# A decoder layer on one core: separate instruction orders for ramp, loop and drain, earlier loads of x, and the split of the norms moved to GpSimd

## The reference

```python
# 1. linear attention, 16 heads of 16, 64 random features
q, k, v = split(x @ Wq.T + bq), split(x @ Wk.T + bk), split(x @ Wv.T + bv)
def phi(u):                       # norm: the squared norm of each head's q or k
    norm = sum(u * u) / (2 * sqrt(16))
    return (exp(u @ orf.T / 16 ** 0.25 - norm) + 1e-6) / 8
kv, ksum = phi(k).T @ v, phi(k).sum(rows)
attn = (phi(q) @ kv) / (phi(q) @ ksum) @ Wo.T + bo
x = layernorm(x + attn)
# 2. softmax attention: queries from ctx_1024, keys x, values ctx_1024
x = layernorm(x + softmax_attention(k=ctx_1024, q=x, v=ctx_1024))
# 3. gated FFN with ternary weights and 8-bit activations
x = layernorm(x + bitlinear(silu(bitlinear(x, w_gate)) * bitlinear(x, w_up), w_down))
```

## Time and profile before

| | |
|---|---|
| median of three runs | 504.94 us |
| the profiled execution | 507.6 us |
| its span, first to last instruction | 505.9 us |
| mean granted TensorE clock | 0.972 |
| busy: TensorE / VectorE / ScalarE / GpSimd | 86% / 89% / 85% / 72% |
| tiles | 32 |

### The profile page before, as it was taken

One profiled execution on the slowest core, in us unless ns is written; L12 is line 12 of the kernel. 1 busy time (PEld: TensorE's weight loads), 2 busy tenths in 40 slices (PEclk: granted clock), 3 DMA queues, 4 the chain that ended last, 5 costly groups with the idle time before them and its releaser, 6 DMA issues.

```text
span 505.9 us, 18665 instructions
## 1 busy us (share of the span) xinstructions
PE 437.2 (86%) x6566; PEld 304.7 (60%) x6566; DVE 450.7 (89%) x1355; ACT 429.1 (85%) x908; POOL 365.0 (72%) x789
## 2 busy tenths in 40 slices
PE   4568888889899999999999999999999988866541
PEld 2235666666677667677767776777777766543220
DVE  4667786889999999999999999999999998999771
ACT  2247788979999999999999999999999998866632
POOL 1447766768888888888888888888888876754332
PEclk9979899999999999999999999999999999999975
DMA  7666556776666666666666666666666777532212
GB/s 180 235 127 110 121 125 116 110 136 94 137 136 140 137 142 138 139 140 145 145 145 145 145 135 141 136 138 143 137 140 130 136 137 138 76 74 53 54 42 62
DMA packets 192644, 64.07 MB, mean 127 GB/s; under 512 B 172384, under 2 KB 192352, under 8 KB 192608
## 3 DMA queue, kind: packets, MB, share of 16 engines
q1 hardware_dynamic: 190080, 60.46, 58.2%
q10 hardware_dynamic: 2528, 3.15, 1.7%
HBM read 17.31 MB, written 4.19 MB: 43 GB/s over the span
## 4 chain that ended last, share of the span: by engine, by line
PE 56%; ACT 15%; DMA 11%; DVE 7%; issue 5%; POOL 3%; SPq 1%; ACTq 0%; POOLq 0%; DVEq 0%
PE bank L1129 11%; PE bank L1333 8%; PE bank L1360 4%; PE bank L1304 3%; PE bank L1181 3%; PE bank L1223 3%; DMA tT<-pkT 3%; DMA ffn_ld<-in_L_ffn_w_down_dram 3%; ACT pT L629 3%; PE bank L1143 3%; ACT pT L628 2%; DMA tT<-nmT 2%; PE bank L1238 2%; PE bank L1320 2%; ACT x L556 2%
## 5 line engine op out<-in xcount | busy, mean ns | idle before, releaser
L1129 PE MATMUL bank<-wq_hi,xT 128*128 128x512 f16 (+1 forms) x256 | 72.1, 337 | 4.0 <-DVE vv L814 2.6
L432 POOL TENSOR_TENSOR ve<-mv,lneps 128x1 f32<-128x1 f32 x96 | 19.2, 200 | 67.8 <-DVE mv L864 52.7
L436 POOL TENSOR_TENSOR rs<-ve,mhalf 128x1 f32<-128x1 f32 x96 | 54.7, 569 | 0.0
L628 ACT ACTIVATE pT<-bank 128x512 f32<-128x512 f32 x64 | 37.9, 592 | 12.6 <-PE bank L1294 10.6
L944 DVE SCALAR_TENSOR_TENSOR g<-th,bank 128x512 f32<-128x512 f32 x64 | 42.9, 671 | 3.9 <-ACT th L651 3.7
L556 ACT ACTIVATE x<-y,nmr,rs 128x256 f32<-128x256 f32 x64 | 39.8, 621 | 7.4 <-DVE y L1005 3.8
L895 DVE TENSOR_REDUCE negm<-bank 128x4 f16<-128x512 f32 x64 | 43.5, 679 | 2.8 <-PE bank L1258 2.7
L896 DVE TENSOR_REDUCE negm<-bank 128x4 f16<-128x512 f32 x64 | 43.6, 681 | 0.0
L1360 PE MATMUL bank<-downT,hqT 128*128 128x256 bf16 x256 | 34.3, 279 | 10.3 <-DMA hqT<-hq 10.3
L575 ACT ACTIVATE phk<-bank 128x512 f32<-128x512 f32 x64 | 39.3, 616 | 4.6 <-PE bank L1148 4.6
L1129 PE MATMUL bank<-wq_lo,xT 128*128 128x256 f16 (+1 forms) x128 | 43.0, 336 | 0.0
(11 more groups left out here) (184 smaller groups left out, 1574.7 us busy)
## 6 DMA issues: line engine op xcount, KB each, us to landing
xs<-in_x_dram SPq DMA_DIRECT2D x32, 128.0 KB, 2.2
cs<-in_ctx_dram SPq DMA_DIRECT2D x32, 128.0 KB, 2.2
xr<-in_x_dram SPq DMA_DIRECT2D x32, 128.0 KB, 2.2
out_dram<-ot SPq DMA_DIRECT2D x32, 128.0 KB, 1.8
ffn_ld<-in_L_ffn_w_gate_dram ACTq DMA_DIRECT2D x1, 1024.0 KB, 8.7
ffn_ld<-in_L_ffn_w_up_dram ACTq DMA_DIRECT2D x1, 1024.0 KB, 11.5
ffn_ld<-in_L_ffn_w_down_dram ACTq DMA_DIRECT2D x1, 1024.0 KB, 13.7
pkAT<-pkA SPq DMA_TRANSPOSE x64, 3.2
```

The source lines that it names most:

```text
L436: g.tensor_tensor(rs[n - 1][:, :], ve[n - 1][:, :], mhalf[:, :], ALU.pow).then_inc(done[f"pw{n}"], 1)
L628: sc.activation(pT[:, grp, 0, :, :], even.rearrange("p (c t) -> p c t", c=4), ACT.Exp, scale=0.25)
L1129: last = T.matmul(o, xT[:, 2 * part + c, :], w[:, c, cols], start=(n == 0), stop=(n == 5))
```

## The change

Seven things change together.

1. `run` takes three functions per engine. `ramp(i)` and `drain(i)` call the steps through `lead(step, i, lag, until)` and `trail(step, i, lag, since)`, each in an order of its own; `iteration` keeps a third order for the loop and two iterations ahead of it. The ramp goes up to tile 13 or so, the loop to tile 29 or so.
2. The loop's order changes on every engine, and the lags of some steps become one smaller (for example `phk0` on TensorE from 3 to 2, `x1_` on ScalarE from 5 to 4).
3. `nhi` and `nlo` go from VectorE to GpSimd.
4. SyncE issues x of tile 0 first, then the projection weights, then x of tile 1, the biases, the output weight and its bias, and the gate matrix. `w_down` and `w_up` follow on SyncE too, after the load of x of tile 3, which waits for `xlo` of tile 1. ScalarE issues none of them any more.
5. VectorE clears all its buffers at the start, ahead of `wq_lo`; the first `wq_lo` comes before the wait for the small weights.
6. The PSUM banks are assigned anew, and the waits that guard them are written for the new orders: by tile number in ramp and drain (`only_at`), in the loop by `wait_looped`. In TensorE's loop the waits of `qkm`, `vm`, `xTp`, `st0`, `kvs`, `s0`, `tm` and others name other steps than before.
7. Steps that lacked a semaphore get one (`s1`, `hq0`), and waits on them are added.

```diff
-            def iteration(i, par): ... run(eng, iteration, lags, first)
+        def run(eng, ramp, iteration, drain, ramps, first, last, drains):
+            for i in range(*ramps):
+                ramp(i)
+            iteration(first - 2, 0)
+            iteration(first - 1, 1)
+            with eng.Fori(first, last - 1, 2) as i:
+                iteration(i, 0)
+                iteration(i + 1, 1)
+            for i in range(*drains):
+                drain(i)
...
+            def load_first(t):
+                sp.dma_start(xs[:, t, :], x[t]).then_inc(moved["x"][t], 16)
+
+            load_first(0)
             for n, w in enumerate((Wq, Wk, Wv)):
                 sp.dma_start(wld[:, n, :, :], w.rearrange("(o p) i -> p o i", p=P)).then_inc(w_in[n], 16)
+            load_first(1)
...
+            def ramp(i):                                # SyncE
+                once(load_gate, i, -78)
...
+                once(load_output, i, -94)
...
+                lead(load_x, i, -68, 16)
...
+                once(load_down, i, -65)
+                lead(load_c, i, -64, 13)
+                once(load_up, i, -65)
...
+                lead(kT, i, -65, 14)
...
+            def nhi(t, par):                            # GpSimd
+                wait_ahead(pool, t, par, ("nr", 0), landings=(("kT", -1), ("qT", -1),))
+                g.tensor_scalar(norm_hi, nrm[:, :, :], 1.0, 0.0, ALU.mult, ALU.add).then_inc(done["nhi"], 1)
+
+            def nlo(t, par):
+                wait(pool, "nhi", t)
+                g.tensor_tensor(norm_lo, nrm[:, :, :], norm_hi, ALU.subtract).then_inc(done["nlo"], 1)
...
             def iteration(i, par):                      # GpSimd
...
+                go(rs3, i, par, 11)
+                go(phe, i, par, 3)
+                go(nf, i, par, 1)
+                go(rs2, i, par, 7)
+                go(chi, i, par, 4)
+                go(clo, i, par, 4)
+                go(nhi, i, par, 1)
+                go(xb_, i, par, 3)
+                go(rs1, i, par, 4)
+                go(lo, i, par, 1)
+                go(nlo, i, par, 1)
...
             def iteration(i, par):                      # VectorE
+                go(bs1, i, par, 4)
+                go(rd, i, par, 3)
+                go(y1, i, par, 4)
+                go(at, i, par, 3)
+                go(am, i, par, 7)
+                go(y3, i, par, 10)
+                go(ac, i, par, 7)
+                go(hc, i, par, 8)
+                go(ar, i, par, 7)
+                go(hr, i, par, 8)
+                go(qnt, i, par, 7)
+                go(hs, i, par, 8)
...
+            def ramp(i):                                # VectorE
...
+                once(magnitudes[2], i, -9)
...
+                lead(qk_, i, -10, 12)
...
+                once(magnitudes[0], i, -11)
...
+                once(magnitudes[1], i, -9)
...
+                lead(nr, i, -10, 12)
...
             def iteration(i, par):                      # ScalarE
...
+                go(ot_, i, par, 11)
+                go(p1, i, par, 6)
+                go(nT_, i, par, 3)
+                go(p0, i, par, 6)
+                go(x2_, i, par, 7)
```

More of the change, by code:

```diff
@@ L263, in wait_ahead, with looping, wait_looped, only_at @@
                     eng.wait_ge(semaphore, v)
+        def looping(t):
+            return not isinstance(t, int)
+        def wait_looped(eng, name, t, off=0):
+            if looping(t):
+                eng.wait_ge(done[name], t + off + 1)
+        def only_at(eng, t, tile, name, producer_tile):
+            if isinstance(t, int) and t == tile:
+                eng.wait_ge(done[name], producer_tile + 1)
+        def lead(step, i, lag, until):
+            t = i - lag
+            if 0 <= t < until:
+                step(t, t % 2)
+        def trail(step, i, lag, since):
+            t = i - lag
+            if since <= t < TILES:
+                step(t, t % 2)
         def go(step, i, par, lag):
             t = i - lag
-            if not isinstance(t, int) or 0 <= t < TILES:
-                step(t, (par + lag) % 2)
+            step(t, (par + lag) % 2)
         def once(step, i, at):
@@ L490, in iteration @@
+            def iteration(i, par):
                 go(xhi, i, par, 0)
+                go(xlo, i, par, 0)
                 go(rs3, i, par, 11)
-                go(rs1, i, par, 5)
-                go(xqf, i, par, 8)
-                go(lo, i, par, 2)
-                go(hq0, i, par, 9)
-            run(pool, iteration, 11, 12)
+                go(phe, i, par, 3)
[8 more added lines that the diff above has]
+                go(nlo, i, par, 1)
+                go(xqf, i, par, 7)
+                go(hq1, i, par, 8)
+                go(hq0, i, par, 8)
+                go(ya2, i, par, 6)
@@ new lines, in drain @@
+            def drain(i):
+                trail(hq0, i, -31, 22)
+                trail(ya2, i, -33, 24)
+                trail(xlo, i, -40, 30)
+                trail(xb_, i, -36, 27)
+                trail(phe, i, -37, 27)
+                trail(chi, i, -36, 26)
+                trail(rs3, i, -29, 19)
+                trail(rs2, i, -33, 23)
+                trail(nf, i, -39, 29)
+                trail(xhi, i, -41, 30)
+                trail(nhi, i, -39, 29)
+                trail(clo, i, -36, 26)
+                trail(nlo, i, -39, 29)
+                trail(lo, i, -39, 29)
+                trail(rs1, i, -36, 26)
+                trail(xqf, i, -33, 23)
+                trail(hq1, i, -32, 22)
@@ L499, in _ @@
+            run(pool, ramp, iteration, drain, (-49, -13), 16, 30, (-11, 3))
         @block.scalar
@@ L559, in x1_ @@
             def x1_(t, par):
+                wait(act, "rs1", t)
                 wait(act, "ya2", t, -2)
@@ L1060, in iteration, with drain @@
                 go(gl1, i, par, 7)
                 go(hu0, i, par, 7)
+                go(sd, i, par, 8)
                 go(hu1, i, par, 7)
                 go(tlo, i, par, 4)
-            run(dve, iteration, 9, 12)
+                go(hh1, i, par, 7)
+                go(ad3, i, par, 8)
+                go(hh0, i, par, 7)
+                go(nr, i, par, 0)
+                go(ad1, i, par, 3)
+                go(hx, i, par, 7)
+            def drain(i):
+                trail(gl0, i, -7, 23)
+                trail(bs2, i, -8, 24)
+                trail(hu0, i, -7, 23)
+                trail(gl1, i, -7, 23)
+                trail(y3, i, -5, 20)
+                trail(v_, i, -14, 30)
+                trail(y2, i, -8, 24)
+                trail(hu1, i, -7, 23)
+                trail(tlo, i, -10, 26)
+                trail(hh0, i, -7, 23)
+                trail(ad3, i, -6, 22)
+                trail(hh1, i, -7, 23)
+                trail(nr, i, -14, 30)
+                trail(hx, i, -7, 23)
+                trail(ad1, i, -11, 27)
+                trail(hc, i, -7, 22)
+                trail(am, i, -8, 23)
+                trail(hr, i, -7, 22)
+                trail(bs1, i, -11, 26)
+                trail(ac, i, -8, 23)
+                trail(rd, i, -12, 27)
+                trail(hs, i, -7, 22)
+                trail(y1, i, -11, 26)
+                trail(ar, i, -8, 23)
+                trail(at, i, -12, 27)
+                trail(qnt, i, -8, 23)
+                trail(bs3, i, -6, 21)
+                trail(qk_, i, -15, 30)
+                trail(m0, i, -10, 25)
+                trail(rx, i, -9, 24)
+                trail(sg, i, -8, 23)
+                trail(oxn, i, -9, 24)
+                trail(m1, i, -10, 25)
+                trail(vsm, i, -13, 28)
+                trail(sd, i, -7, 22)
+                trail(kve, i, -13, 28)
@@ L1067, in _ @@
+            run(dve, ramp, iteration, drain, (-16, 2), 14, 30, (15, 27))
         @block.tensor
```

794 lines of the change are left out of this document (549 added, 245 removed), and 6 rows, old and new, of the table done.

## The result

The changed kernel takes 511.5 us (median of 4 runs, 509.59 to 513.66) against 505.23 us for the kernel before on the same chip: a ratio of 1.0126, 95% interval 1.0092 to 1.016. It is slower by 1.3%. The prediction of 487 us (473 to 500) is wrong in size and in sign. The profiled execution took 510.29 us with a span of 508.6; before it was 507.6 with 505.9.

A forecast was written before the change was run, and what follows sets the result against it. It took a throughput-bound loop with three full engines, and two ends bound by latency and step order. 507.6 - 5.4 - 1.0 (VectorE at the ends) - 2.5 - 6.0 - 3.5 = 489.2, median 487 us; range 473 to 500.

The forecast's parts named there:

- The loop: Tiles between ramp and drain: period falls from 13.05 to 12.80 us over 21.5 tiles, -5.4 us (0 to -8.6).
- The floor of 12.65 us: Loop: ScalarE's own work per tile, 13.05 less 0.40 us of waits; VectorE's floor falls to 12.64 us.
- Rival (a): The loop keeps its 13.05 us period because TensorE is full too; 492 us, chance 0.15.
- `nhi` and `nlo` on GpSimd: Loop: about 0.25 us each, 0.5 us a tile, hidden in GpSimd's wait for `y1`, cost on the path 0.
- Rival (c): Loop: slower because GpSimd, with the added `nhi` and `nlo`, becomes the bound; 518 us, chance 0.08.
- The start: Before the first tiles: earlier x load, first `qk_` near 16 us, FFN loads on SyncE delay `kT`; -2.5 us (+1 to -6).
- The ramp: From 20 to 120 us: new order removes about a quarter of VectorE's and ScalarE's idle time, -6 us (-1 to -11).
- The drain: After 400 us: new order removes waits such as the last `x2_` for `ad3`, -3.5 us (0 to -7).

The follow-up runs named there:

- e4: The changed kernel with one more wait: in the loop GpSimd's `lo` also waits for VectorE's `qnt`; 502.38 us, ratio 0.9957 to the kernel before.
- e12: Small kernel without the decoder layer: four VectorE instructions alone, then beside a GpSimd subtract of `lo`'s shape; two go from 0.35 and 0.42 to 1.15 to 1.29 us.
- e13: e10 with the third of three passes of both projections left out on TensorE; period 13.09 us.
- e3: The kernel before with only `nhi` and `nlo` moved to GpSimd, ahead of `rs1`; 506.64 us, ratio 1.0046.
- e8: e4 with the output weight's transposes and their copy moved later and VectorE's first and third reductions swapped at the start; 500.8 us, ratio 0.9922.
- e9: e8 with the three FFN loads issued from ScalarE as before the change; 499.9 us, ratio 0.9905.
- e10: e8 with the wait of `lo` for `qnt` in ramp and drain too, not only in the loop; 500.5 us, ratio 0.9921.
- e5: The changed kernel with `nhi` and `nlo` back on VectorE, `lo` still ahead of `xqf`; 527.15 us, ratio 1.0435.

## Why the prediction was wrong, point by point

- **The loop, -5.4 us: wrong, this is the failed step.** It was +12.1 us between tiles 8 and 28. The step asked what each engine has to do and which waits an order can remove. It never asked what two engines do at the same instant: it put the overlap of `qnt` with `lo` at nothing, without a row for it. "GpSimd gains `nhi` and `nlo`, cost on the path 0" went through what is queued behind them, and named `lo` and `xqf`, but not that the diff also changed which of the two comes first. The changed kernel's own tiles, e4 and e12 show the collision, and it is the whole of the loss: `qnt` takes 1.32 us instead of 0.35 in twelve tiles, each of these is 1.0 to 1.2 us longer than the spared ones, the period is 13.64 us instead of the 12.80 forecast, and with the two kept apart (e4) the span is 6.9 us shorter than before instead of 2.7 longer.
- **The floor of 12.65 us: right as arithmetic, but no run came down to it.** The pitches came as said (`hc` 0.13 instead of 0.24 us, `hr` 0.08 instead of 0.17, `nhi` and `nlo` gone), but other places opened: `hx` to the next start 0.17 (0.12 and 0.23 in turn) instead of 0.06, `nr` to the next start 0.42 instead of 0.33. Rival (a) was right in size for the kernels without the collision, 13.08 against its 13.05, and its reason ("TensorE is full too") was not: e13 takes 0.65 of 13.08 us of TensorE's work away for nothing. These kernels hold my wait for `qnt`, which is a link of the circle; a loop with neither that wait nor the collision was not tried. The nearest to it are the four spared tiles of the changed kernel at 12.87 to 12.89 us, close to the 12.80 forecast. What holds the kernel before at 13.05 us stays open.
- **`nhi` and `nlo` on GpSimd, 0.25 us each: 0.33 and 0.35 to 0.40 us.** Somewhat more, and covered as said: GpSimd's wait for `y1` shrank. Rival (c), slower through GpSimd, had the right sign for another reason: not GpSimd's load, but the moment of its start. e3 rules its mechanism out.
- **The start, -2.5 us: size nearly right (-1.4 at `ad1` of tile 0), path wrong.** The first `qk_` came at 18.05, not 16, since the output weight on TensorE stood ahead; I had named `magnitudes[0]` as what is late next, and that came after it. The gate matrix landed at 15.8 instead of 14 us. The first matmul of the key features came 3.1 us earlier (26.08 against 29.20 us), for 2.5 said. With the first `qk_` at 12.28 us (e8) it came 5.9 us earlier with the FFN loads on SyncE, and 6.2 with them on ScalarE (e9): the 6 us were to be had in either queue, so the reason given for losing 3.5 of them was wrong.
- **The ramp, -6 us: about right.** Start and ramp together 7.7 us at tile 8, for 8.5 forecast. VectorE's idle time from 20 to 120 us went only from 21.7 to 19.4 us, where I had said 16; the work done in the stretch, 1356 matmuls for 1239, shows the gain better.
- **The drain, -3.5 us: 1.7 us.** Half the size. VectorE's idle time after 400 us did not fall to 18 us: it was 22.3 of 108 us, against 21.4 of 106.
- **The range** ended at 500 us, with 0.08 for slower, and no case in it in which a part of the change costs more than it brings, but GpSimd's load. A change of the order of three engines needed such a case.

A better version than both kernels came out: e9 at 499.9 us, 0.9905 of before (0.9874 to 0.9935), with e8 and e10 within 1 us of it. Of the 13.4 us between it and the 486.5 us forecast, 5.4 are the loop term, which none of these kernels shows; the rest is at the two ends: one gap between two `ad1` at the end of the ramp's order is still 14.2 to 14.3 us in all three.

## What to carry to other kernels

When an order on GpSimd or VectorE changes, list the pairs of the two engines' instructions that will newly run at the same time, and look in the trace whether a SBUF to SBUF instruction of VectorE ever overlapped one of GpSimd; here one wait that keeps them apart was worth 9 us. When some tiles of a loop collide and others do not, compare the two kinds within one trace: that is the cleanest price. When an engine is as busy as before with fewer instructions, compare the median and maximum duration of each line, not the busy share. And three engines at 99% are no proof of a bound by load: leave work out of one, then of all; if the period stays, look for the circle of waits.

## What the runs showed of the hardware that I had not expected

VectorE's instruction can be held until GpSimd's has ended: 0.35 becomes 1.15 to 1.36 us beside an instruction of 1.15 us, and every held `qnt` of the changed kernel ends 0.15 us after `lo`. Of such a pair just one is held, and which one can't be told from the starts that the profile records: in tiles 6 and 14 of the changed kernel alike `lo` starts 0.05 us behind `qnt`, and in tile 6 `qnt` takes 1.35 us, in tile 14 `lo` takes 1.32. The two outcomes have very different prices: 0.16 us more on GpSimd and no longer period, or 1.0 us more on VectorE and as much on the period. In the loops of the kernel before and of e4 `lo` started 1.03 and 0.42 us after `qnt`, when that was done, and neither was stretched.

The Trainium skill (SBUF — State Buffer, Who interferes with whom) says that VectorE and GpSimd share a pair of SBUF interfaces as an exclusive lock; that the one which comes first has it for its whole instruction; and that `tensor_scalar` in its two-port mode, and any VectorE instruction with two SBUF inputs while GpSimd reads SBUF, fall under it, but not reductions. The pairs of e12 agree: 1.15 to 1.23 and 1.29 us beside, and the reduction's 0.42 unchanged. The `tensor_scalar` that reads PSUM is not held either (0.48), a case that this section does not name by itself. It is the rule that spoke against this change, and the prediction did not weigh it.

The reverse case stands in the trace of the kernel before: beside two of VectorE's weight preparations (128x2048, there 1.77 and 1.85 us) `nf` took 1.57 us instead of 0.73.

The same small move has another price in another place: `nhi` on VectorE took 0.09 us of pitch in the kernel before, and up to 1.08 us in e5, where it met `lo`.
